# A reordered opening, a last result in halves, and four checked pieces in halves in a one-core attention and gated-layer kernel

## What is computed

```python
xn = _layernorm(x)
# branch 1 (cut): conv, norm, projections, q/k elu, kv, out projection, conv, norm, MLP
# branch 2, each _tlin is einsum('bsi,oi->bso', x, w) * s with w in {-1, 0, 1}
h = silu(_tlin(xn, w1, s1)) * _tlin(xn, w2, s2)      # 256 -> 1024
h = gelu(_tlin(h, h1, ...)); h = gelu(_tlin(h, h2, ...))   # 1024 -> 1024, twice
ffn = _tlin(h, w3, s3)                                # 1024 -> 256
out = x + attn_block(xn) + ffn
```

## Time and profile before

| | |
|---|---|
| median of 3 runs | 1075.15 us (1072.56 to 1079.33) |
| profiled execution | 1074.53 us, of which the span of the trace is 1072.7 us |
| PE / DVE / ACT / POOL busy | 96% / 71% / 56% / 22% |
| first matmul | 11.1 us after the span's start |
| last matmul | ends 1068.0 us, 4.7 us before the span's end |

### The profile page before, as it was taken

One profiled execution on the slowest core, in us unless ns is written; L12 is line 12 of the kernel. 1 busy time (PEld: TensorE's weight loads), 2 busy tenths in 40 slices (PEclk: granted clock), 3 DMA queues, 4 the chain that ended last, 5 costly groups with the idle time before them and its releaser, 6 DMA issues. The chain is left out here.

```text
span 1072.7 us, 17199 instructions
## 1 busy us (share of the span) xinstructions
PE 1027.1 (96%) x6644; PEld 910.2 (85%) x6644; DVE 759.4 (71%) x956; ACT 603.7 (56%) x874; POOL 238.4 (22%) x214
## 2 busy tenths in 40 slices
PE   3899999999999999999999999999999999999997
PEld 3678877888877777877788889999899999999997
DVE  6884689534548568988887657867787968776664
ACT  4678667676444364655655535555655654655444
POOL 3444255224305021111001031222200211101100
PEclk9999999999998999999999999999999999999999
DMA  8978615966784635423322473243494423222210
GB/s 303 422 238 338 219 52 178 331 209 206 261 289 142 198 126 207 160 97 109 127 79 79 156 295 117 86 134 118 148 367 174 157 79 119 90 77 87 103 40 22
DMA packets 68402, 180.68 MB, mean 168 GB/s; under 512 B 5040, under 2 KB 26160, under 8 KB 64688
## 3 DMA queue, kind: packets, MB, share of 16 engines
q1 hardware_dynamic: 68320, 179.56, 48.1%
HBM read 121.86 MB, written 66.06 MB: 175 GB/s over the span
## 5 line engine op out<-in xcount | busy, mean ns | idle before, releaser
L2226 PE MATMUL pr<-xp_hi,wb 128*128 128x256 f32 x1344 | 320.0, 282 | 0.9 <-DVE u L1978 0.7
L2226 PE MATMUL pr<-xp_lo,wb 128*128 128x256 f32 x1344 | 319.5, 281 | 0.0
L2226 PEld LDWEIGHTS pr<-xp_hi,wb 128*128 128x128 f32 x1344 | 255.3, 190 | 2.7 <-issue 2.7
L2226 PEld LDWEIGHTS pr<-xp_lo,wb 128*128 128x128 f32 x1344 | 255.8, 190 | 0.0
L2226 PE MATMUL pr<-u_hi,ring 128*128 128x512 f32 x256 | 102.5, 400 | 1.8 <-POOL u_lo L931 1.0
L2226 PE MATMUL pr<-u_lo,ring 128*128 128x512 f32 x256 | 100.0, 391 | 0.0
L1416 ACT CAST xp_hi<-tf 128x1024 fp32r<-128x1024 f32 x48 | 50.2, 1046 | 56.4 <-PE pr L2226 19.9
L1050 POOL TENSOR_TENSOR ot<-ot,yg 128x512 f32<-128x512 f32 x14 | 25.2, 1802 | 244.3 <-DVE ot L2009 244.3
L1831 DVE TENSOR_TENSOR h_lo<-hf,h_hi 128x512 fp32r<-128x512 f32 x64 | 54.6, 862 | 32.6 <-ACT h_hi L1356 32.6
L2411 PE MATMUL pr<-wf_hi,h_hi 128*128 128x256 f32 x256 | 75.3, 294 | 0.6 <-DVE h_lo L1831 0.6
L1972 DVE TENSOR_TENSOR xp_lo<-tf,xp_hi 128x1024 fp32r<-128x1024 f32 x48 | 60.8, 1266 | 20.2 <-ACT xp_hi L1416 20.1
(11 more groups left out here) (230 smaller groups left out, 2526.7 us busy)
## 6 DMA issues: line engine op xcount, KB each, us to landing
ring<-w_s SPq DMA_DIRECT2D x42, 512.0 KB, 7.4
uf<-h_s SPq DMA_DIRECT2D x16, 1024.0 KB, 5.1
wb<-s_s SPq DMA_DIRECT2D x8, 1024.0 KB, 9.2
wb<-w_s SPq DMA_DIRECT2D x6, 1024.0 KB, 9.9
vw<-v_s SPq DMA_DIRECT2D x8, 514.0 KB, 6.8
xt<-x SPq DMA_DIRECT2D x8, 512.0 KB, 6.0
xn_s<-xh SPq DMA_DIRECT2D x8, 512.0 KB, 9.6
stage<-w_gated SPq DMA_DIRECT2D x2, 2048.0 KB, 13.5
```

The lines of the kernel that those rows point to most:

```text
L2226: return e.matmul(bank, w.bitcast(dt), v_.bitcast(dt), start=first, stop=last, skip_group_check=True)
```

## The change

Opening: `load_x(0)` is issued ahead of the parameters, and DVE waits for the parameters only after the first two tiles are applied; the order on DVE is now moments 0, apply 0, moments 1, apply 1. `load_xg(0)` is gone; both parts of the first gated input are made from `xh[0]`, on ACT between `split_attn_weights` and `conv1_centre(1)`, on POOL ahead of `inverse_deviation(0, "b")`. On ACT `apply_norm(0)` comes ahead of `apply_xn(2)`, and `high_of_norm(0)` and `copy_xn(2)` ahead of `apply_xn(3)`. On DVE one of three full checks ahead of `low_of_norm(0)` moves behind it. The pieces 7 to 10 are checked in halves, one half (128x512) behind each of the eight gating products; the last piece stays full at the end of step -1. The last result of the last tile is made in halves all the way, and the last `down` starts with the first half. The `checked` counts grow by four.

```diff
+HALVED = 7
+FIRST_CHECKS = STREAM + KH // 2
...
+            load_x(0)
             sp.dma_start(prm[:], t["params"]).then_inc(s["prm_in"], 16)
-            load_x(0)
             sp.dma_start(ident[:], consts[:, 0:P]).then_inc(s["prm_in"], 16)
...
-            load_xg(0, xg1)
             save_xn(1)
...
             halo(1, xh, "xh_w", 1, "xh_halo")
+            low_of_xg(0, xg1_lo, mid(xh[0]), xg1_hi)
+            inverse_deviation(0, "b", "b_applied")
             inverse_deviation(2, "a", "a_applied")
-            inverse_deviation(0, "b", "b_applied")
             inverse_deviation(3, "a", "a_applied")
             halo(2, xh, "xh_w", 1, "xh_halo")
-            low_of_xg(0, xg1_lo, xg1, xg1_hi)
             inverse_deviation(1, "b", "b_applied")
...
+                if i == 2:
+                    e.wait_ge(s["x_split"], 1)
                 e.copy(mid(xh[i % 2]), X[:]).then_inc(s["xh_w"], 1)
...
             split_attn_weights()
+            high_of_xg(0, xg1_hi, mid(xh[0]))
             conv1_centre(1)
+            apply_norm(0)
             apply_xn(2)
-            apply_norm(0)
-            apply_xn(3)
             high_of_norm(0)
             copy_xn(2)
-            high_of_xg(0, xg1_hi, xg1)
+            apply_xn(3)
             xi_out(0)
...
+            def last_result(h):
+
+                t_, before = BLOCK_RUNS + TILES - 1, len(RESULTS) * (TILES - 1)
+                e.wait_ge(s["u_sum"], 5 * t_ + 5 + h)
+                for m in range(2 * h, 2 * h + 2):
+                    last = e.activation(results[3][:, m, :], u2[:, m, :], ACT.Gelu,
+                                        scale=par("h2_s", RESULTS[3][0] * HB + m))
+                last.then_inc(s["c_gelu"], 1)
+                e.wait_ge(s["c_gelu"], gelus(t_, 3) + 2 * h)
+                e.wait_ge(s["down_mm"], before + 1)
+                e.copy(a_hi[3][:, 2 * h:2 * h + 2, :], results[3][:, 2 * h:2 * h + 2, :]).then_inc(s["c_gelu"], 1)
...
         @block.vector
         def _(e):
-            e.wait_ge(s["prm_in"], 32)
...
+            def check_half(m):
+
+                n, part = HALVED + m // 2, slice(m % 2 * PIECE // 2, (m % 2 + 1) * PIECE // 2)
+                e.wait_ge(staged(CHECK_ORDER[n]), 16)
+                e.wait_ge(s["checked"], HALVED + max(m, 1))
+                e.scalar_tensor_tensor(out=acc[:, part], in0=stage(CHECK_ORDER[n])[:, part].bitcast(I32), scalar=0xFFF,
+                                       in1=acc[:, part], op0=ALU.bitwise_and, op1=ALU.bitwise_or).then_inc(s["checked"], 1)
...
                         e.wait_ge(s["h1_mm"], KH * j)
 
+                        if j == 0:
+                            check_half(m)
...
             xn_moments(0)
+            apply_xn(0)
             xn_moments(1)
-            apply_xn(0)
             apply_xn(1)
+            e.wait_ge(s["prm_in"], 32)
+            conv1_side(0, False)
             check_staged(range(0, 1))
-            conv1_side(0, False)
             conv1_side(0, True)
             xn_moments(2)
             norm_moments(0)
             xn_moments(3)
             norm_offsets(0, "b", "b_applied")
-            check_staged(range(1, 2))
             low_of_attn_weights()
-            check_staged(range(2, FIRST_LAYER))
+            check_staged(range(1, 3))
             low_of_norm(0)
+            check_staged(range(3, FIRST_LAYER))
+            staged_bits(0, FIRST_LAYER)
             conv1_side(1, False)
-            staged_bits(0, FIRST_LAYER)
             conv1_side(1, True)
...
-                if i < 0:
-                    check_staged(range(7, 8))
...
-                if i < 0:
-                    check_staged(range(8, 9))
...
-                if i < 0:
-                    check_staged(range(9, 10))
...
                 if i < 0:
-                    check_staged(range(10, STREAM))
-                    staged_bits(1, STREAM)
+                    e.wait_ge(staged(CHECK_ORDER[STREAM - 1]), 16)
+                    check(FIRST_CHECKS, stage(CHECK_ORDER[STREAM - 1]), acc)
+                    staged_bits(1, FIRST_CHECKS)
...
+            def last_result_21(h):
+                t_, part = BLOCK_RUNS + TILES - 1, slice(2 * h, 2 * h + 2)
+                e.wait_ge(s["prod"], NP * t_ + 7)
+                e.wait_ge(s["u_sum"], 5 * t_ + 4)
+                e.tensor_tensor(u2[:, part, :], quarters(pr[1])[:, part, :], u2[:, part, :], ALU.add) \
+                    .then_inc(s["u_sum"], 1)
+
+            def low_of_last_result(h):
+                part = slice(2 * h, 2 * h + 2)
+                e.wait_ge(s["c_gelu"], gelus(BLOCK_RUNS + TILES - 1, 3) + 1 + 2 * h)
+                e.tensor_tensor(a_lo[3][:, part, :], results[3][:, part, :], a_hi[3][:, part, :].bitcast(F32), ALU.subtract) \
+                    .then_inc(s["a_lo"], 1)
...
+            def last_down(wide):
+
+                half, tokens = RESULTS[3]
+                for c in range(HB):
+                    e.wait_ge(s["a_lo"], len(RESULTS) * (TILES - 1) + 4 + c // 2)
+                    for i in range(2):
+                        for n, v_ in enumerate((a_hi[3], a_lo[3])):
+                            last = add(as_tokens(down_banks)[:, 2 * tokens + i, :], v_[:, c, i * P:(i + 1) * P],
+                                       wd[:, half * HB + c, :], wide, False, c == HB - 1 and n == 1)
+                last.then_inc(s["down_mm"], 1)
```

More of the change, by code:

```diff
@@ L1495, in _ @@
                 for k, ps in ((1, ()), (2, (4, 5)), (3, (6,))):
-                    gelu_block(t_, k)
-                    high_of_result(r, k)
+                    if k == 3 and not more:
+                        for h in range(2):
+                            last_result(h)
+                    else:
+                        gelu_block(t_, k)
+                        high_of_result(r, k)
                     if more:
@@ L1857, in check_late @@
                 sums = late_sum[u % 2][:].rearrange("p (a b) n -> p a (b n)", a=2)
-                check(STREAM + 2 + checks_before(u) + n, sums[:, n, :], acc2)
+                check(FIRST_CHECKS + 2 + checks_before(u) + n, sums[:, n, :], acc2)
             def check_late2(t, n):
```

34 lines of the change are left out of this document (21 added, 13 removed).

## The result

The changed kernel takes **1066.32 us** (median of 5 runs, 1063.59 to 1067.48), the kernel before in the same comparison 1074.77 (5 runs, 1072.56 to 1079.33). The ratio is 0.9918, with a 95% interval of 0.9893 to 0.9943: about 0.8% faster. The profiled execution took 1063.92 us with a span of 1062.1 us.

What follows compares the result with a forecast made beforehand. PE, busy 96% of the span, was taken as the bound; 1.2 (in_proj(0)) - 1.15 (halves) + 1.4 (last result) gave 1.5 us gained, so 1073.6 us from the median 1075.15; range 1068.8 to 1077.2.

Steps and rivals of the forecast that it cites:

- The start, 0.15 us: Opening, tiles 0 and 1: tile 1's transposes start at about 14.1 against 14.24, 0.15 us gained, inside later waits.
- `in_proj(0)`, 1.2 us: Opening: one check fewer on DVE frees POOL's tile 2 offsets earlier; in_proj(0) starts at 33.0, 1.2 us gained.
- not held: Upper end for in_proj(0): POOL's small operations are not held by DVE, 3.07 us gained.
- The clock at `in_proj(0)`, 0: First products at in_proj(0) run at the 1.2 GHz level; cost left as it is, about 1.2 us more if not.
- The first gated input, 0: First gated product: the way through DRAM was covered, so removing it is worth 0, at most 0.4 us lost.
- Halves, 1.15 us lost: Up to the second flag: half checks wait behind POOL's low parts and delay norm_back(1); 1.15 us lost on balance.
- rival (a): At norm_back(1): norm_offsets(1) gets in ahead of POOL's low part; stretch costs nothing, 2.6 us gained, 1072.5 us; chance 0.25.
- DVE's tail: DVE from last gating to the second flag's reduction end: half, check, two POOL low parts and 1.22; again 5.0 us.
- nothing collides: Upper end for the halves: the 0.88 us gating wait and the 0.83 us at the flag are gained, 1.71 us.
- work well behind 70 us moving: Sign against the prediction: it is wrong if work well after 70 us moves; no size given.
- The last result, 1.4 us: End of the kernel: in halves, PE goes straight on into the last down without idling, 1.4 us gained.

Runs made afterwards that it cites:

- e8: Changed kernel with the old start: parameters loaded first and waited for, moments 0 and 1 ahead of both applies; 1066.95 us, one run.
- e11: Changed kernel with one wait added on DVE, so checks 1 and 2 start after POOL's offsets of tile 2; 1065.78 us, ratio 0.9931.
- e1: Changed kernel unaltered, measured and traced again, against the kernel before at 1074.22 us; 1066.22 us, ratio 0.9928.
- e3: Changed kernel with the last result made whole, as before; 1067.39 us, ratio 0.9934.
- e4: Changed kernel with pieces 7 to 10 checked whole in their old places; 1067.03 us, ratio 0.9938.
- e13: The kernel of e4 (changed kernel, pieces 7 to 10 checked whole) traced a second time; 1067.7 us.
- e14: The kernel of e4 (changed kernel, pieces 7 to 10 checked whole) traced a third time; 1069.29 us.
- e7: Changed kernel with the first gated input saved to DRAM and loaded back again; 1067.81 us, one run.
- e5: Changed kernel with ACT normalising tile 3 ahead of the cast of pb_hi again; 1069.04 us, one run.
- e6: Changed kernel with POOL's deviation of tile 2 ahead of that of the norm of tile 0 again; 1067.32 us, one run.
- e12: Kernel before with only pieces 7 to 10 checked in halves behind the gatings; 1071.52 us, one run.
- e2: Kernel before with only the last result made in halves; 1071.66 us, ratio 0.9983.
- e9: Kernel before, unaltered, for a second trace; 1074.57 us.

## Why the prediction was wrong, step by step

The sum was 1.5 us and the medians differ by 8.0 to 8.5. Its largest error is the halves, put at 1.15 us lost and worth 1.44 gained: the loss needed `norm_offsets(1)` to be caught behind POOL's low part, and it was not. Then come `in_proj(0)`, sized 1.2 where 2.7 came, the falling clock behind the flag, which had no term (1.5), and the clock at `in_proj(0)`, put at nothing (0.9). The last result was right.

**The start, 0.15 us: mis-sized.** The first transpose of tile 1 was forecast at 14.1 and came at 13.92. But I took the transposes as the measure, and the start has a second consumer: the sides of the first convolution, which DVE does in the new order ahead of its check. With the old start `in_proj(0)` is 1.1 us later (e8). The step that failed is the inference from PE's transposes, which barely move, to a gain of 0.15 us. The 1.1 us hold for the new order; against the kernel before, DVE's chain came only 0.3 us earlier.

**`in_proj(0)`, 1.2 us: the mechanism right, the size 2.7.** POOL's small operations are held by DVE, as I said: in the changed kernel the last one, at 26.03, takes 1.09 us and ends at 27.12, with DVE's first check, and with the checks out of its way it takes 0.20 (e11). What I did was to shift the end of POOL's block by one operation, 1.22 us, for the one check less. The rows that I should have walked through are these, POOL before (the fourth is in the earlier trace rows):

```profile
24.85 1.16 POOL L889 TENSOR_TENSOR rs_a<-mv_a,small 128x4 f32<-128x4 f32 x1 [0.39 <-DVE mv_a L1515]
26.09 1.39 POOL L891 TENSOR_TENSOR rs_a<-rs_a,small 128x4 f32<-128x4 f32 x1
27.46 1.10 POOL L894 TENSOR_SCALAR nb_h<-mv_a 128x4 f32<-128x4 f32 x1
```

and the same four operations, POOL after:

```profile
24.11 0.20 POOL L892 TENSOR_TENSOR rs_a<-mv_a,small 128x4 f32<-128x4 f32 x1
24.39 1.02 POOL L894 TENSOR_TENSOR rs_a<-rs_a,small 128x4 f32<-128x4 f32 x1
25.39 0.56 POOL L897 TENSOR_SCALAR nb_h<-mv_a 128x4 f32<-128x4 f32 x1
26.03 1.09 POOL L900 TENSOR_TENSOR nb_h<-nb_h,rs_a 128x4 f32<-128x4 f32 x1
```

against DVE's block after:

```profile
24.45 1.41 DVE L1583 SCALAR_TENSOR_TENSOR wq_lo<-wa_raw,prm,wq_hi 128x512 fp32r<-128x512 f32 x2
...
25.84 2.55 DVE L1595 SCALAR_TENSOR_TENSOR acc<-stage,acc 128x1024 int32<-128x1024 int32 x2
```

Most POOL operations that meet the block end within 0.1 us of a DVE instruction's end (before, the first, third and fourth: 26.01, 28.57 and 29.87 against 25.95, 28.48 and 29.81); the second is held as well, 1.39 us for 1.02. Before, all four were held, behind the moments of tile 3 (mv_a, done at 24.77). Tile 2's moments had long been done, so after the change the first operation came 0.74 us earlier, ahead of the block, and was not held (0.20), and the second had begun before it and ran beside it (1.02). By operation: 0.74 earlier start, then 0.96, 0.37, 0.54 and 0.13 us shorter, together 2.74, and 29.87 - 27.12 = 2.75. The check that held the first operation before (DVE, 24.73 to 25.95) is the one that the change moved out of the block. All else follows at the same distance: ACT's apply 29.90 to 27.15, the cast 31.88 to 29.13, `in_proj(0)` 34.23 to 31.48. My bound for "not held" (3.07) was sound as a bound; the value between the bounds was chosen by the one row of 1.22 us, and the nearest end would have been better. Timeline of ACT in the changed kernel:

```profile
27.15 2.07 ACT L1061 ACTIVATE xt<-xt,nb_h,rs_a 128x256 f32<-128x256 f32 x4 [0.66 <-POOL nb_h L900]
29.13 0.99 ACT L1145 CAST pb_hi<-pr 128x1024 fp32r<-128x1024 f32 x1
```

**The clock at `in_proj(0)`, 0: it gave 0.9 us on average.** The products' spacing shows the level: 0.43 us at 1.2 GHz, 0.23 at 2.4, as the rows at a granted clock of 0.50 and 1.00 have it. From `in_proj(0)` to the 81st matmul the seven traces with the old opening take 6.79 to 8.15 us (mean 7.63), the seven with the new one, its order unaltered (after, e1, e3, e4, e13, e14, e7), 6.33 to 7.50 (mean 6.77). In e11, where PE waited 0.45 us ahead of it, all products run at 0.23 and it takes 5.51. I had said that this would be up to 1.2 us more if the stretch did not start slow, and gave it no value. The two groups overlap, and the three changed kernels whose `in_proj(0)` starts at 32.46 to 34.12 (e5, e6, e8) take 7.08 to 7.47, so that the new opening is what brings the 0.9 us is likely and not shown.

**The first gated input, 0: right against the kernel before.** The transfer was covered, and the old opening with the input through DRAM has the same stretches as the new one without it (e7, e12). What I left out is what it would cost in the new opening, 0.75 us: I looked at where POOL's low part would be put, and not at whom it would hold where it had been. The 0.75 us are a loss that the edit prevents, and no term of the sum.

**Halves, 1.15 us lost: 1.44 gained.** This is the step with the wrong sign. The collision that I described is there: the half at 44.40 waits for POOL's low part. But `norm_offsets(1)` went in ahead of POOL's next one, rival (a). DVE and POOL in the changed kernel (two timelines):

```profile
43.02 0.69 DVE L1609 SCALAR_TENSOR_TENSOR acc<-stage,acc 128x512 int32<-128x512 int32 x1
...
44.40 1.16 DVE L1609 SCALAR_TENSOR_TENSOR acc<-stage,acc 128x512 int32<-128x512 int32 x1
45.49 0.15 DVE L1558 SCALAR_TENSOR_TENSOR nb_b<-mv_b,rs_b 128x4 f32<-128x4 f32 x1
```

```profile
43.71 1.30 POOL L934 TENSOR_TENSOR u_lo<-full,u_hi 128x512 fp32r<-128x512 f32 x1 [0.17 <-ACT u_hi L1192]
45.59 1.29 POOL L934 TENSOR_TENSOR u_lo<-full,u_hi 128x512 fp32r<-128x512 f32 x1 [0.58 <-ACT u_hi L1192]
```

POOL's low part ends at 45.01, the half at 45.56: it needs 0.55 us once released, where I had put its full 0.7. The same holds further on: the half at 49.06 ends 0.56 behind POOL's part (48.76 + 1.29), the one at 53.82 ends 0.54 behind (53.13 + 1.30). With 0.7 it would have ended at 45.71, and the small operation would have asked behind POOL at 45.59; with 0.55 it is ahead by 0.10 us. In e12 the margin is 0.13, the stretch 26.07 to 26.13 us in eight traces, so it is a narrow order but a steady one.

The second error is the price of that rival, 0. By the marks on PE: from the 81st matmul to `norm_back(1)` 0.24 us lost (9.59 to 9.83), from there to the gating product that used to stall 1.10 gained (6.50 to 5.40, of which 0.88 is the listed wait), and from it to the flag's small matmuls 0.58 gained (10.39 to 9.81). I had let every delay reach the reduction. In fact PE arrived early, not late: DVE's last gating ends 20.22 us behind the 81st matmul (58.05 - 37.83), before 21.39 (62.41 - 41.02), so 1.17 us of the 1.44 were gained ahead of it. DVE's tail from there to the reduction's end, put at 5.0 us, is 62.72 - 58.05 = 4.67, before 4.94: of the last rows of DVE after

```profile
58.08 1.14 DVE L1609 SCALAR_TENSOR_TENSOR acc<-stage,acc 128x512 int32<-128x512 int32 x1
59.33 2.14 DVE L1595 SCALAR_TENSOR_TENSOR acc<-stage,acc 128x1024 int32<-128x1024 int32 x1
61.50 1.22 DVE L1614 TENSOR_REDUCE bits<-acc 128x1 f32<-128x1024 int32 x1
```

the half and the check each waited once for POOL, 1.4 us together against 1.1 of the two checks in 3.65 us before, but there is half a check less to do. The Trainium skill, page "SBUF — State Buffer", section "SBUF: two separate sides", lets the one that starts first keep the shared ports for its whole instruction, and a half check waits behind a whole low part: the trace agrees (1.16, 1.55 and 1.14 us against 0.69 unheld). What I made of it was too much: each collision moved DVE, and only the one at `norm_back(1)` showed on PE, as a loss of 0.24 us up to there.

One reading of the bound was wrong too: "nothing collides" counted the 0.83 us at the flag as time to gain. That is the time in which the flag is made and read, 0.82 to 0.86 us in all eighteen traces; what could be gained there is PE's wait for the reduction ahead of it, 0.88 us, of which 0.59 went.

**The last result, 1.4 us: right.** 1.45 us in e2, 1.34 between the two profiled traces. PE had no wait ahead of the last `down`, and from DVE's last add to the span's end it was 10.4 us (forecast 10.8; 12.2 before). Of the last 0.4 us nothing is the change's: from PE's last matmul to the span's end the traces differ by themselves, 4.2 to 6.3 us.

**The flag's clock, not in the sum.** Three of four traces of before lose about 1.5 us behind the second flag; the one that the prediction was made from is the fourth. I had no row for it. I had written that work well behind 70 us moving would prove me wrong, and this is such work.

**The sum again.** By the means of the traces: 34.14 - 31.47 = 2.67 for `in_proj(0)` (with the start in it), 0.86 for the clock behind it, 1.44 for halves, 0 for the first gated input, 72.40 - 70.93 = 1.47 behind the flag (four traces of before, eight new ones with halves), 337.35 - 335.99 = 1.36 at the end: 7.8 us, against 8.0 measured in e1's comparison. The middle gives 588.2 in seven old traces and 587.5 in eleven new ones, 0.7, with spreads of 3.6 and 2.9 within each group; that isn't told from none.

Of this, `in_proj(0)`, the halves and the end, 5.5 us, are each shown by a kernel with that part alone or with it undone. The two terms of the clock, 2.3 us, are differences of means whose cause is not shown.

## What to carry to other kernels

Where small operations of one engine queue against long ones of another, walk them one by one, and count how many long instructions each has to pass: what brings the first of them ahead of the block is worth a whole instruction, and one row can't show it. An edit that is worth nothing against the old kernel may be what a faster one needs: test it in both, and ask whom its helper operation holds in each. And read a clock-dependent stretch in more than one trace before calling its length the kernel's own: here one trace of four was the exception, and the prediction was made from it.

## What the runs showed of the hardware that was not expected

- A held DVE instruction ends 0.54 to 0.56 us behind its release, where the same 128x512 check takes 0.69 us unheld: 0.13 to 0.15 us of it are not spent again after the wait.
- POOL's second small operation (L894 in the changed kernel, 1.02 us) ran from 24.39 beside DVE's two weight operations (24.45, 1.41 for both) and lengthened neither: 1.01 to 1.04 us and 1.41 us are also their lengths elsewhere (POOL's at 23.14, DVE's before at 25.87, where POOL's operation was held). The Trainium skill, page "SBUF — State Buffer", section "SBUF: two separate sides", has an exclusive lock for the whole instruction; by it DVE, with two inputs in SBUF, would have had to wait until POOL's operation ended at 25.41. The trace does not agree: no wait shows.
- The number of slow products at `in_proj(0)` changes from one execution to the next of the same kernel: some 6 in the first trace of before and some 12 in e9, and 6.79, 7.94, 8.05 and 8.08 us to the 81st matmul in the four. The Trainium skill, page "TensorE: Matmul & The Clock Gate", section "Part 1: The HAM clock gate", says that the count of slow matmuls at a kernel's start varies by run; the traces agree for this start after a wait.
- A granted clock of 1.00 in a window can mean that nothing is recorded there. In e9 the row below gives 1.00 for 34 to 36 us, while five matmuls fill the 2 us and the products stand 0.43 us apart, which is the 1.2 GHz level. The trace's first entry of the clock is its rise at 39.3 us, just where the spacing goes to 0.23; ahead of the first entry the windows print 1.00.

```profile
34.00:36.00 2.00, 2.00 (x5) 1.61 (x6) 2.00 (x3) 0.95 (x1) 0.97 (x1) 1.00 1.04 422
```

  The spacing of equal matmuls tells the level where the record doesn't.
